# Two graph-attention layers: the feed-forward of layer 0 and the projection of layer 1 as one stage

## The reference

```
q, k, v = split(layer_norm(x, g1, be1) @ w_qkv)          # 8 heads of 16
scores  = where(adj != 0, q @ k.T * SCALE, -inf)
out     = softmax(scores) @ v
x       = x + out @ w_proj + b_proj
h       = layer_norm(x, g2, be2)
x       = x + gelu(h @ w1 + b1) @ w2 + b2                # 512 hidden columns
```

## Time and profile before

| | |
|---|---|
| median of 3 runs | 3417.16 us (3416.44 to 3418.13) |
| profiled execution | 3420.91 us, its span 3419.1 us |
| mean granted TensorE clock | 0.956 of full |
| busy: PE, DVE, ACT, POOL | 3282.7, 2741.2, 2431.9, 2535.7 us |
| the stages that the change touches | 1640 to 1890 us of the span |

### The profile page before, as it was taken

How to read it: one execution, slowest core, us unless ns; L and a number is a source line. 1 busy time by engine, 2 the same in 40 slices (tenths; PEclk the granted TensorE clock), 3 DMA queues, 4 the chain that set the end, 5 groups by cost and what they waited for, 6 DMA issues and landing times.

```text
span 3419.1 us, 71112 instructions
## 1 busy us (share of the span) xinstructions
PE 3282.7 (96%) x22152; PEld 1439.7 (42%) x22152; DVE 2741.2 (80%) x8790; ACT 2431.9 (71%) x3557; POOL 2535.7 (74%) x1532
## 2 busy tenths in 40 slices
PE   6999999999999999999769999999999999999988
PEld 3434344444434343432544444444444444444326
DVE  6888888888889898880338899999999999999514
ACT  3279797878888797968322577777777777777753
POOL 3178878787878788789221588888888888888960
PEclk8699999999999999999876799999999999999989
DMA  8687887879787879774247656565656566565522
GB/s 231 205 273 231 274 256 250 265 236 286 234 286 225 292 221 289 237 250 137 81 104 184 179 153 196 160 188 166 187 169 183 172 180 175 178 179 174 145 87 72
DMA packets 502485, 683.05 MB, mean 200 GB/s; under 512 B 60896, under 2 KB 282464, under 8 KB 502112
## 3 DMA queue, kind: packets, MB, share of 16 engines
q1 hardware_dynamic: 501824, 678.40, 65.6%
q10 hardware_dynamic: 288, 0.10, 0.0%
HBM read 514.17 MB, written 164.10 MB: 198 GB/s over the span
## 4 chain that ended last, share of the span: by engine, by line
PE 83%; issue 6%; DVE 3%; DMA 2%; SPq 2%; POOL 2%; ACT 1%; POOLq 1%; DVEq 0%; ACTq 0%
PE PS L578 28%; PE PS L561 20%; PE PS L585 17%; PE PS L591 14%; DVE spill L931 2%; PE PS L506 1%; POOL arena L1121 1%; PE PS L639 1%; DMA q_t<-max_dram 1%; ACT arena L823 1%; POOLq L1083 1%; DMA mask<-in_adj_t 1%; PE PS L709 0%; PE PS L518 0%; SPq L356 0%
## 5 line engine op out<-in xcount | busy, mean ns | idle before, releaser
L931 DVE CUSTOM_DVE_ANT_0 spill<-PS,mask_n 128x512 bf16<-128x512 f32 x4096 | 2592.0, 687 | 326.3 <-PE PS L561 318.8
L823 ACT ACTIVATE arena<-PS 128x512 f32<-128x512 f32 (+1 forms) x3072 | 2133.4, 739 | 618.6 <-PE PS L585 374.9
L1121 POOL TENSOR_TENSOR arena<-arena,mask 128x1024 int32<-128x1024 int32 x896 | 2132.7, 2380 | 426.8 <-ACT arena L823 362.7
L561 PE MATMUL PS<-k_t,q_t 48*128 48x512 f32 x4096 | 1660.5, 535 | 21.8 <-issue 8.6
L585 PE MATMUL PS<-q_t,k_t 50*128 50x512 f32 x4096 | 1258.5, 485 | 14.2 <-DMA q_t<-max_dram 11.4
L591 PE MATMUL PS<-arena,idb 64*128 64x512 bf16 x4304 | 1151.5, 389 | 0.0
L578 PE MATMUL PS<-arena,v_sb 128*32 128x512 f32 x8192 | 1095.7, 607 | 9.1 <-POOL arena L1121 8.6
L561 PEld LDWEIGHTS PS<-k_t,q_t 48*128 48x128 f32 x4096 | 605.4, 192 | 954.6 <-DVE pmax L931 882.4
L585 PEld LDWEIGHTS PS<-q_t,k_t 50*128 50x128 f32 x4096 | 594.5, 188 | 213.1 <-issue 118.0
L591 PEld LDWEIGHTS PS<-arena,idb 64*128 64x128 bf16 x4304 | 310.7, 94 | 375.2 <-PE PS L591 229.2
L931 DVE DVE_READ_ACCUMULATOR2_ANT pmax<- 128x1 f32 x4096 | 340.0, 83 | 0.0
(11 more groups left out here) (56 smaller groups left out, 734.4 us busy)
## 6 DMA issues: line engine op xcount, KB each, us to landing
mask<-m_dram SPq DMA_DIRECT2D x768, 256.0 KB, 2.8
mask_n<-mn_dram SPq DMA_DIRECT2D x768, 128.0 KB, 2.8
adj_in<-in_adj SPq DMA_DIRECT2D x256, 256.0 KB, 4.4
mask<-in_adj_t SPq DMA_DIRECT2D x256, 256.0 KB, 4.0
m_dram<-mask SPq DMA_DIRECT2D x256, 256.0 KB, 3.7
mn_dram<-mask_n SPq DMA_DIRECT2D x256, 128.0 KB, 4.4
mt_dram<-arena SPq DMA_DIRECT2D x256, 128.0 KB, 3.6
arena<-mt_dram SPq DMA_DIRECT2D x256, 128.0 KB, 2.8
```

The lines of the kernel that those rows point to most:

```text
L561: pe.matmul(ps_a[:, (L * NSC + n) % A_BANKS, :], q_t[r0:r0 + KROWS, gb % Q_SLOTS, pair, q * P:(q + 1) * P], k_t[r0:r0 + KROWS, pair, mb * ...
L823: nc.scalar.activation(p_buf[:, t % P_SLOTS, heads, :], ps_b[:, heads, :], ACT.Exp, scale=SCALE).then_inc(exped[part], 1)
L931: dve.tensor_tensor_reduce(spill[:, bank, :], ps_a[:, bank, :], mask_n[:, v % N_SLOTS, :], 1.0, LOWEST, ALU.subtract, ALU.max, pmax[:, p % ...
L1121: pool.tensor_tensor(p, p, m, ALU.mult).then_inc(p_masked, 1)
```

## The change

`feed_forward(0)` and `project(1)` become one stage, `feed_and_project(0)`, without a barrier between them. It has NB + 1 = 9 iterations. Iteration g does the feed-forward of block g, the projection of block g - 1, and 16 score tiles: in iteration g these are the second half of the tiles of K's block g - 3 and the first half of those of block g - 2. The first 8 tiles stand in iteration 2, and 24 tiles are left behind iteration 8.

What goes with it:

- x of layer 1 isn't read back from DRAM: `norm_stats` and POOL's `norm_rows` read `x3`, the feed-forward's result, which has two buffers now. The normalised rows and their turned copies have four buffers (NORMS) instead of two, in all stages.
- PSUM: the hidden columns, K, Q and V of the joint stage share banks 4 and 5 in turn (`JOBS`, `job_bank`; `job_turn` waits for the user before the last), and the first 128 score tiles of layer 1 have two banks (`a_bank`) instead of three. Layer 0 and the last feed-forward keep their banks.
- SP's list of the joint stage is sorted by new numbers, and the 707 KB of feed-forward weights of layer 1 are loaded at the start of `attend(1)` instead of inside `project(1)`.

The core of the diff (the functions of SP and POOL are rewritten in the same sense):

```diff
+            def feed_and_project(L):                      # TensorE
+                gi0, M = L * NB, L + 1
+
+                def score_late(g, i):
+                    score_block(M, *((g - 3, i + 4) if i < 4 else (g - 2, i - 4)))
...
+                for g in range(NB + 1):
+                    gp = M * NB + g - 1
+                    if g < NB:
+                        gx = ORDER["f", L, g]
+                        hidden(gi0 + g, gx, 0)
+                        score_late(g, 0)
+                        hidden(gi0 + g, gx, 1)
+                        if g + 2 < NB:
+                            turn_o(gi0 + g + 2)
+                        score_late(g, 1)
+                        hidden(gi0 + g, gx, 2)
+                        score_late(g, 2)
+                        hidden(gi0 + g, gx, 3)
+                        score_late(g, 3)
+                        second_layer(gi0 + g, 0)
+                        if g + 2 < NB:
+                            turn_attn(gi0 + g + 2)
+                        score_late(g, 4)
+                        second_layer(gi0 + g, 1)
...
+                for n in range((NB - 2) * NS * 4 + 8, NB * NS * 4):
+                    score_a(M, n)
...
+            def feed_and_project(L):                      # VectorE
...
+                for g in range(NB + 1):
+                    take_block(g, 0, 2)
+                    if g + 2 < NB:
+                        normalise(gi0 + g + 2)
+                    take_block(g, 2, 5)
+                    if g < NB:
+                        add_ff(gi0 + g)
+                        norm_stats(x3[:, g % 2, :].rearrange("p (t c) -> p t c", t=NS), ORDER["p", M, g])
+                    take_block(g, 5, 6)
+                    if g + 2 < NB:
+                        add_attention(gi0 + g + 2, ORDER["f", L, g + 2])
+                    take_block(g, 6, 8)
...
+                order = [(g - 2.75, "o", g) for g in range(NB)]         # SyncE
+                order += [(g - 2.6, "x", g) for g in range(NB)]
+                order += [(g + 0.6, "y", g) for g in range(NB)]
+                if L + 1 < LAYERS:
+                    order += [(g + 1.85, "k", g) for g in range(NB)]
+                    order += [(g + 1.9, "q", g) for g in range(NB)]
+                    order += [(g + 2.05, "K", g) for g in range(NB)]
+                    order.append((2.1, "Q", 0))
+                    order += [(v // NS + 0.25 * (v % NS) + 1.5, "r", v) for v in range(NS * NC)]
```

455 lines of the change are left out of this document (305 added, 150 removed).

## The result

The changed kernel takes 3427.43 us (median of 20 runs, 3424.10 to 3438.12), the kernel before 3415.54 us (20 runs, 3411.98 to 3427.64) on the same chip: ratio 1.0031, interval 1.0024 to 1.0039. It is 12 us slower; the forecast was 11 us faster (3406 us). The time is inside the range of 3380 to 3430 us, its sign is not the one that was given 0.61.

The account below looks back on a forecast made before the run. TensorE and DVE were taken as nearly level, their waits for each other deciding. The stage summed to 236.5 us against 250, attend(1) took 2 back, 11.5 less than 3417.2: 3406 us, range 3380 to 3430.

Parts of the forecast that it names:

- The stall in a full iteration: Iterations 3 to 5, behind add_attention: TensorE idle 5.8 us in one piece, DVE waiting over 2 us for POOL's root.
- The clock term: Full iterations: the clock falls in the 5.8 us gap; slow matmuls behind it cost 1.9 us (1.1 to 3.2).
- About 1.4 of waiting for score banks: Full iteration, before the second layer's second half ends: TensorE waits about 1.4 us for score banks while DVE normalises.
- Iteration 2: First scores: K and Q take 14 us through DRAM, TensorE waits some 7; the iteration 29.5 us (23 to 33).
- Iterations 0 and 1: Start of the joint stage: 10 us without projection or scores, then 17.5 with projection and a late DVE.
- The tail: Iteration 8 and last tiles: 16 us until K is stored, 9.5 its way, 16 tiles at 0.79; 36 us.
- attend(1): Start of attend(1): 707 KB of weights ahead of the first mask rows cost 2 us (0 to 5).
- POOL's rows beside DVE's add: add_attention: its first add would wait up to 0.8 us beside POOL's rows, 5 us in all; left out.
- the rival in which the clock holds: Joint stage: clock stays up and loads are in time; 3384 us, 33 less with attend(1); chance 0.20.
- The signs: Iterations 3 to 5 start 25 to 28 us apart; sum wrong if stage's end is over 20 us off 1876.
- The slower one: Joint iterations: clock stays at the lower level; 3457 us, or 3440 for two thirds of the time; chance 0.17.
- The rival of no change: Interlocking costs 2 us more in each of six iterations, above all K's loads landing late; 3417 us; chance 0.16.

Follow-up runs that it names:

- e1: Changed kernel with two maxima moved inside add_attention, before the wait for POOL's root, in iterations 2 to 5; ratio to the kernel before 0.9983.
- e4: Changed kernel with five unused matmuls filling most of TensorE's gap in each of iterations 2 to 5; ratio to the kernel before 1.0027.
- e6: Changed kernel with SyncE's loads of attention output and residual placed behind the K and Q loads; ratio to the kernel before 1.0032.
- e2: Changed kernel with POOL taking both roots of an iteration before the projection's rows; ratio to the kernel before 1.0016.
- e5: Changed kernel with bank 5 as a third score bank for the last 24 tiles; ratio to the kernel before 1.0020.
- e7: Kernel before, with only two score banks instead of three for layer 1's first 128 tiles; ratio to the kernel before 1.0070, stage 274.7 us.
- e3: Changed kernel with layer 1's 707 KB of feed-forward weights loaded some 40 steps into attend(1); ratio to the kernel before 1.0029.
- e9: Changed kernel with a third score bank from iteration 6 on, hidden columns, K, Q and V using banks 1 and 2; ratio to the kernel before 1.0026.

## Why the prediction was wrong

The mechanism was the one that was walked through: each wait stands where it was said to stand. What failed is the step from the waits to their sizes: the sum was 21.5 us short (the stage: 236.5 forecast, 258.0 measured), by five terms that all erred to the same side. The largest is the full iteration, 26.5 us forecast and 28.5 measured in the mean of three.

| term | forecast | measured | difference |
|---|---|---|---|
| lead-in | 26 | 25.6 | -0.4 |
| iteration 0 | 10 | 14.2 | +4.2 |
| iteration 1 | 17.5 | 19.5 | +2.0 |
| iteration 2 | 29.5 | 34.1 | +4.6 |
| iterations 3 to 5 | 79.5 | 85.4 | +5.9 |
| iterations 6, 7 | 38 | 37.8 | -0.2 |
| iteration 8 and tail | 36 | 41.5 | +5.5 |

- **The stall in a full iteration.** "TensorE is idle for 5.8 us in one piece": 5.98 to 6.31. The wait for POOL's root "over 2 us": 1.94 to 2.26. Right, and e1 shows that it is the place that decides. The clock term of 1.9 us was near (2.1 by e4).
- **"About 1.4 of waiting for score banks".** This step failed in iterations 3 to 5. The walk came to 24.6 us at full clock, and the one iteration that had it (e4) takes 26.1. `add_ff` starts 13.7 us into iteration 3, not 11.9; with the full clock of e4 it starts at 12.8, so 0.9 us of the 1.8 is the slow start that the clock term holds, and the other 0.9 is TensorE and DVE waiting for each other over two banks, first DVE for 3.17 us behind the stall and then TensorE for banks. The walk let DVE idle "a little between pairs". If all three iterations are as that one, this step is 4.5 of the 5.9 us, and the rest is the clock.
- **Iteration 2.** The wait for Q was put at some 7 us and is 7.72. The way was taken as 14 us, since the DMAs would be less busy; it is 15.9 where the earlier trace rows has 16.8, and e6 shows that what lies beside it is not its price. I had no row for the shorter way. The first score starts 15.6 us into the iteration and not 13.6. The other 2.6 us of the 4.6 lie behind it and are not settled by an experiment.
- **Iterations 0 and 1.** 3.8 of the 6.2 us is the clock that came back later in this profile than in others; 2 us is POOL's order, which e2 took away. The forecast gave iteration 0 the full clock, as the earlier trace rows has it from 1666 us on (0.98); four of the twelve traces of the joint stage have it so, and the other eight have 0.82 to 0.87.
- **The tail.** The spacing of 0.79 was right (0.80), and so was its cause (e5: 0.61 at the same clock with three banks). The way of K was 10.7 us (store 1865.42, score 1876.15) and not 9.5: the "1.8 until the loads are issued" counts from Q's store in the earlier trace rows, and K's goes out ahead of it, here 2.7 us before the loads (1868.09); K was stored 17.1 and not 16 us into iteration 8, and the 16 tiles took 13.7 us where the sum had 10.5 after a deduction "less what overlaps" that nothing in the trace bore out.
- **The banks as a whole** were priced at 3 us in the tail, next to the 1.4 us per iteration and the stall that two full banks make. No term said what the third bank had been worth; e7 puts it at 24 us in the schedule it came from. That it is dear could have been read from the earlier trace rows: the round trip of two maxima at half clock is 1.59 us, and `project(1)` is at half clock most of the time.
- **attend(1).** 2 us forecast; 2.4 at the first maximum, and 3.0 in all by the means of the traces (e3).
- **POOL's rows beside DVE's add** were left out of the sum. The pair exists and costs 0.2 to 0.6 us at each meeting (last section).
- **Two readings** were off without weight for the result. The 9.4 us before 1785.03 is the gap between two weight loads; between the matmuls it is 8.6. And the rival in which the clock holds is 32 us less with `attend(1)`, not 33.
- **The signs.** The gaps (5.98 to 6.31 us), the wait for Q (7.72) and the spacing of the last maxima (0.80) came as named. The iterations 3 to 5 took 28.2, 27.8 and 29.5 us and not 25 to 28, and the wait ahead of the last 16 tiles was 3.12 and not about 5. The sign of a wrong sum came too: counted from the stage's own start, its end is 21.5 us late, more than the 20 that were named.
- **The rivals.** The slower one, a clock that stays down, did not come: 0.86 in iterations 3 to 5. The rival of no change named the right kind of cause, 2 us more of interlocking in each of six iterations, and stopped at no change, with K's loads as its ground, which have no part in iterations 3 to 5. A rival with the forecast's mechanism and every term at its upper end (iteration 2 at 33, the tail at 42, the clock at 3.2) would have stood at 26 + 10 + 17.5 + 33 + 3 x 27.8 + 38 + 42 = 250 us for the stage, level with the one before and 2 us slower with `attend(1)`; the chance of slower lay all on the clock instead.

Measured against the old stage: the change takes 34 us of empty time out and gives it back as four stalls of 6 us with slow matmuls behind them, a wait of 7.7 us, and two waits for K and a bank's round trip in the tail. What is left open is how the 24 us of e7 divide in the new schedule; e5 and e9 bound only the part from iteration 6 on, at 3 to 4 us. No run gives the iterations 2 to 5 a third bank, so nothing shows whether that would have removed the stall as e1's order did; and none takes the four buffers of normalised rows, or x that isn't read again, by itself.

## What to carry to other kernels

When two stages are laid into each other, the piece of a list that may not be interrupted matters more than the sum of work: find the longest run of instructions on one engine between two releases of the other, compare it with what the buffers between them hold (here two tiles, 1.2 us, against 7 us of `add_attention`), and put releases inside it before anything is fused. A buffer that is given away is priced where it is used at the slowest clock, not where it looks idle. And where a sum of waits is made, let one rival be the same story with all terms at their upper ends: here the errors of interlocking all fell to one side.

## What was not expected of the hardware

POOL's short instruction grows when it meets a DVE addition of two SBUF operands. POOL and DVE in iteration 1 of the changed kernel:

```profile
1671.61 0.79 POOL L1313 TENSOR_SCALAR arena<-arena 128x4 f32<-128x4 f32 x1 [12.28 <-DVE arena L1112]
...
1676.90 0.23 POOL L1313 TENSOR_SCALAR arena<-arena 128x4 f32<-128x4 f32 x1
```

```profile
1671.62 0.69 DVE L1237 TENSOR_TENSOR arena<-arena,wts 128x512 f32<-128x512 f32 x1
```

0.79 us instead of 0.23, started 0.01 us before DVE's; DVE kept its 0.69. Two such meetings stand in each of the twelve traces of the joint stage. The two engines start within 0.01 us of each other, now the one ahead and now the other, and each time POOL's instruction takes 0.78 or 0.79 us and DVE's 0.69. POOL's times in a profile are rough, but no other instruction of this form in these stages takes more than 0.25. The four rows beside such an addition took 3.36 us (1742.66) and, in e2, 3.77, against 3.14 in the earlier trace rows. SBUF — State Buffer in the Trainium skill (section "SBUF: two separate sides") says that whichever of the two starts first has the pair of ports for its whole instruction and the other one blocks. The traces agree that one of them waits for about the other's length, but in this row it is POOL, by the records the first to start, that was held up.

The clock of TensorE at the start of the stage did not follow from the program: iteration 0, with the same instructions, had a mean granted clock of 0.82 to 0.87 in eight profiles and 1.00 in four, 13.6 to 14.4 against 11.8 us.
